# Whole tiles of adj by turns on two DMA queues, in place of half tiles on both

## The chip, the cores and the metric

The kernel runs on one core of one Trainium2 chip. The metric is the device time of one execution in microseconds (us), lower is better. The core has TensorE (PE in the profile, its weight loads PEld), VectorE (DVE), ScalarE (ACT), GpSimd (POOL) and SyncE (SP). Transfers are issued by SyncE, ScalarE and GpSimd, each into a queue of its own (q1 is SyncE's, q10 ScalarE's), and 16 DMA engines carry them out.

## What is computed

Two graph layers over N = 4096 nodes with 128 features, both with the same dense 4096 x 4096 float32 matrix adj (64 MB) and a layer norm ahead:

```python
h = jnp.maximum(_layernorm(x, axis=-1), 0.0)
x = x + _L0_gnn_ref(h, adj, L0_gnn_weight, L0_gnn_bias)
h = jnp.maximum(_layernorm(x, axis=-1), 0.0)
x = x + _L1_gnn_ref(h, L1_gnn_context, adj, ...)

# L0: a hyperbolic layer
h = proj(mobius_matvec(weight, x, C_IN), C_IN)
h = proj(mobius_add(h, hyp_bias, C_IN), C_IN)
support_t = adj @ logmap0(h, C_IN)
h = proj(expmap0(support_t, C_IN), C_IN)
return proj(expmap0(jax.nn.relu(logmap0(h, C_IN)), C_OUT), C_OUT)

# L1: attention over the edges of adj
left, right = in_fts @ w_left + b_left, in_fts @ w_right + b_right
logits = left[:, None] + right[None, :]
logits = jnp.where(logits >= 0, logits, 0.2 * logits)
logits = jnp.where(adj_tensor <= 0.0, -jnp.inf, logits)
return jax.nn.relu(jax.nn.softmax(logits, axis=-1) @ relation)
```

## The kernel before

It works in two parts. The first reads adj once, multiplies with it (layer 0) and keeps only the sign of each entry as an int8 mask in SBUF. The second computes layer 1 from that mask and doesn't touch adj.

The first part goes through NC = 8 chunks of 512 rows of adj (output nodes), and in a chunk through NC = 8 tiles (g = 0 to 7) of 512 columns. A tile is 512 x 512 float32, 1 MB. It is loaded into one of XSLOTS = 4 slots of `loaded` by four transfers of 256 KB, one for each quarter b of the partitions (quarter b is partitions 32 b to 32 b + 31, and takes columns 128 b to 128 b + 127 of the tile). Each transfer reads 512 runs of 512 bytes. `LOW` is quarters 0 and 1 (partitions 0 to 63), `HIGH` quarters 2 and 3 (64 to 127).

When all four have landed (semaphore `adj_in` of the slot), VectorE turns the tile in four blocks with 32 x 32 transposes (L975, `turn_block`, 0.69 us each) into four slots of `turned`. TensorE multiplies each block (L671), and ScalarE takes the signs of two blocks at a time (L829), which counts up `half_signed`. VectorE may overwrite a block's slot when it is multiplied and signed. The slot of `loaded` is free for tile g + 4 when tile g is turned.

Who asks for tile g + 4: SyncE's program `load` (L347) waits for `half_signed` to show tile g signed and then issues quarters 0 and 1 (L354). ScalarE issues quarters 2 and 3 (`load_high`, L719) in its own program, right behind its second sign of tile g, without a wait. The first four tiles of chunk 0 are loaded by SyncE alone, all four quarters in the order 0, 2, 1, 3, and the context (4 MB) after them, also by SyncE. An engine's program goes on when its issue has been taken; while an issue is held back, what stands behind it in that engine's program waits.

Between the tiles stand small transfers of 64 KB: at tile 4 the finished rows of two chunks earlier are stored (`store_x1`, L324), at tile 7 the rows of x for the chunk before are loaded into `xk` (`load_x`, L331), LOW by SyncE, HIGH by ScalarE. GpSimd (L553) waits for xk, and VectorE's statistics (L1093), among the last tile's blocks, wait for GpSimd.

Of the kernel before, what the change touches and what calls it, by code (L numbers as in the profile page):

```python
# [52 lines left out]
XT_AHEAD = 4  # L53
BESIDE = 8
STORE_AT, LOAD_AT = 4, 7
LOW, HIGH = range(NQ // 2), range(NQ // 2, NQ)

MIN_NORM2 = 1e-30
# [20 lines left out]
def bass_two_graph_layers(nc, x, adj, weight, bias, context, w_common, w_left, b_left, w_right, b_right, out):  # L79
# [3 lines left out]
    NC = N // CH  # L83
# [4 lines left out]
    with ExitStack() as ctx:  # L88
# [179 lines left out]
        adj_n = adj.rearrange("(s r p) (g b j) -> s g b p r j", r=CH // Q, p=Q, b=NQ, j=L * Q)  # L268

        def pick(view_, c):  # L270

            if isinstance(c, int):
                return view_[c]
            v = view_[bass.ds(c, 1)]
            names = "abdefg"[:len(v.shape) - 1]
            return v.rearrange(f"z {' '.join(names)} -> (z {names[0]}) {' '.join(names[1:])}")
# [28 lines left out]
        def by_l(t, l, j=None):  # L305

            v = t.rearrange("p (s l) d -> p l s d", l=L)[:, l]
            return v if j is None else v[:, j * L:(j + 1) * L]
# [12 lines left out]
        def store_x1(eng, p, blocks):  # L321
            eng.wait_ge(x1_ready, p + 1)
            for b in blocks:
                eng.dma_start(out_n[p, b], xk[b * Q:(b + 1) * Q]).then_inc(x1_stored, 16)  # L324

        def load_x(eng, p, blocks):
            if p:
                eng.wait_ge(x1_stored, p * (16 * NQ))
                eng.wait_ge(h2_ready, p)
            for b in blocks:  # L330
                eng.dma_start(xk[b * Q:(b + 1) * Q], x_n[p, b]).then_inc(xk_loaded, 16)  # L331
# [4 lines left out]
        @block.sync  # L336
        def _(sp):
            def load_nodes(t, src, into, blocks):
                for l in range(L):
                    for b in blocks:  # L340
                        sp.dma_start(by_l(t, l)[b * Q:(b + 1) * Q], src[l, b]).then_inc(into[l], 16)
            load_nodes(x_in, x_l, x_in_sem, LOW)

            for l in range(L):
                sp.wait_ge(x_in_sem[l], 16 * NQ)

            def load(c):  # L347

                for g in range(NC):
                    first_tiles = c == 0 and g < XSLOTS  # L350
                    if not first_tiles:
                        sp.wait_ge(half_signed, c * TH + HALVES * (g - XSLOTS + 1))
                    for b in (0, 2, 1, 3) if first_tiles else LOW:
                        sp.dma_start(loaded[b * Q:(b + 1) * Q, g % XSLOTS], adj_n[c, g, b]).then_inc(  # L354
                            adj_in[g % XSLOTS], 16)
                    if c == 0 and g == XSLOTS - 1:
                        load_nodes(cx, cx_l, cx_in, range(NQ))
                    if g == STORE_AT and c >= 2:
                        store_x1(sp, c - 2, LOW)
                    if g == LOAD_AT and c >= 1:  # L360
                        load_x(sp, c - 1, LOW)

            def neg_left_row(c, parity):
                sp.dma_start(nl[parity], (nl_dram[c * L:(c + 1) * L] if isinstance(c, int) else
                                          nl_dram[bass.ds(c * L, L)]).rearrange("(a l) p -> a (l p)", a=1)
                             .broadcast_to([P, CH])).then_inc(nl_loaded[parity], 16)

            for c in range(NC):
                load(c)
            sp.wait_ge(nl_stored, 16 * NQ)  # L370

            sp.wait_ge(block_turned, NC * NK - (XSLOTS - 1) * L)
            neg_left_row(0, 0)
            store_x1(sp, NC - 2, range(NQ))
            load_x(sp, NC - 1, range(NQ))

            def rows_out(p):

                os = pick(out_n, p)

                for b in range(NQ):
                    sp.dma_start(x1k[b * Q:(b + 1) * Q], os[b]).then_inc(x1_loaded, 16)
                sp.wait_ge(y_ready, p + 1)
                for b in range(NQ):
                    sp.dma_start(os[b], y[b * Q:(b + 1) * Q]).then_inc(out_stored, 16)

            def chunk_of_phase_2(c, parity):
                sp.wait_ge(parts_ready, c * NC - NC)
                neg_left_row(c, parity)
                rows_out(c - 2)  # L390

            store_x1(sp, NC - 1, range(NQ))
            neg_left_row(1, 1)
            sp.wait_ge(x1_stored, NC * 16 * NQ)
            sp.wait_ge(rest_ready, NK)
            sp.wait_ge(rest0_ready, NC)
            with sp.Fori(1, NC // 2) as pair:
                chunk_of_phase_2(pair * 2, 0)
                chunk_of_phase_2(pair * 2 + 1, 1)
            rows_out(NC - 2)  # L400
            for b in range(NQ):
                sp.dma_start(x1k[b * Q:(b + 1) * Q], out_n[NC - 1, b]).then_inc(x1_loaded, 16)
            for l in range(0, L, 2):
                sp.wait_ge(y_ready, NC + l // 2)
                for b in range(NQ):
                    sp.dma_start(out_n[NC - 1, b][:, l:l + 2], y[b * Q:(b + 1) * Q, l:l + 2]).then_inc(out_stored, 16)
            sp.wait_ge(out_stored, (NC + 1) * 16 * NQ)
# [299 lines left out]
        def _(act):  # L707
# [5 lines left out]
            act.dma_start(b_colv, bias.rearrange("(d a) -> d a", a=1)).then_inc(weights_in, 16)  # L713
            act.dma_start(bias_b, bias.rearrange("(a d) -> a d", a=1).broadcast_to([P, D])).then_inc(weights_in, 16)

            def load_high(rows, g):

                for b in HIGH:
                    act.dma_start(loaded[b * Q:(b + 1) * Q, g % XSLOTS], rows[g, b]).then_inc(adj_in[g % XSLOTS], 16)  # L719

            for l in range(1, L):
# [47 lines left out]
            def bias_part(k):  # L769

                if k >= XT_AHEAD:
                    act.wait_ge(xt_ready, k - XT_AHEAD + 1)
                nc.scalar.activation(fb[:, k % XT_AHEAD, :], hb, ACT.Copy, scale=sv[:, 14, k:k + 1]).then_inc(
                    fb_ready, 1)
# [39 lines left out]
            def signs(c, parity):  # L814
                number = isinstance(c, int)
                acc_of[0] = acc[1 - parity]
                steps = {}
                if c >= 1:
                    copy, squares, tanh, _ = post_steps(c - 1)
                    steps = {0: copy, 4: squares, 9: tanh}  # L820
                if c >= 2:
                    steps[2] = post_steps(c - 2)[3]
                if c == NC - 1:
                    steps[7] = exponentials
                mc = mask[:, c] if number else mask[:, bass.ds(c, 1)].rearrange("p o k i -> p (o k) i")
                for half in range(TH):
                    act.wait_ge(block_turned, c * NK + HB * (half + 1))
                    slots = half % HALVES * HB
                    nc.scalar.activation(mc[:, half * HB:(half + 1) * HB, :], turned[:, slots:slots + HB, :],  # L829
                                         ACT.Sign).then_inc(half_signed, 1)  # L830
                    if number and c == 0:
                        for k in range(XT_AHEAD + half * HB, min(NK, XT_AHEAD + (half + 1) * HB)):
                            bias_part(k)
                    if half in steps:
                        steps[half]()
                    if half % HALVES == HALVES - 1:
                        tile = half // HALVES + XSLOTS
                        if tile < NC:
                            load_high(adj_n[c], tile)
                        elif c < NC - 1:  # L840
                            load_high(adj_n[c + 1], tile - NC)
                        if tile == STORE_AT and c >= 2:
                            store_x1(act, c - 2, HIGH)
                        if tile == LOAD_AT and c >= 1:
                            load_x(act, c - 1, HIGH)
# [6 lines left out]
            for c in range(NC):  # L852
                signs(c, c % 2)
# [414 lines left out]
```

## Time and profile before

| | |
|---|---|
| three timed runs | 627.44, 631.89, 632.68 us; median 631.89 |
| the profiled execution | 626.75 us, its span 625.0 us |
| busy, share of the span | PE 503.0 us (80%), DVE 510.6 (82%), ACT 420.0 (67%), POOL 234.4 (38%) |
| adj loads issued | SyncE 136, ScalarE 120, 256.0 KB each, 9.8 and 9.0 us from issue to landing |
| packets of q1 and q10 | 49.69 MB and 34.35 MB |

Busy times are of the whole program and mix the two parts; a share of the DMA engines above 1 means that the recorded times of packets overlap on an engine. Durations all come from the one profiled execution.

### The profile page before, as it was taken

The numbers are of one execution on the slowest core, as the hardware profiler recorded it, in microseconds if no ns is written. First come the engines' busy times: TensorE is split into PE (matmuls) and PEld (weight loads), VectorE is DVE, ScalarE is ACT, GpSimd is POOL, SyncE is SP. The second block draws the span as 40 slices with busy tenths as digits, with TensorE's granted clock in tenths as the row PEclk, the third lists the DMA queues.
The fourth block names the chain that finished last, engine by engine and source line by source line (L and its number), as shares of the span: only waits on it lengthen the run. The fifth ranks groups of instructions, "written<-read, shape, count | busy, mean of one in ns | idle before, by whom it ended". The sixth has DMA issues, their size and how long they took to land.

```text
span 625.0 us, 8712 instructions
## 1 busy us (share of the span) xinstructions
PE 503.0 (80%) x2695; PEld 313.2 (50%) x2695; DVE 510.6 (82%) x980; ACT 420.0 (67%) x554; POOL 234.4 (38%) x259
## 2 busy tenths in 40 slices
PE   0823999898989878896886565699999999999995
PEld 0721443332423332342332444488787878787874
DVE  3896987766857676683676999999999999999994
ACT  1955876563746446463466958498989898989881
POOL 4820047757556684532333886201111111010100
PEclk9975999998999899899799879989999999999999
DMA  6997999999999999999992010101010101011010
GB/s 151 225 221 145 185 259 282 276 254 274 232 273 240 242 232 239 268 235 194 241 258 71 5 34 1 35 18 35 18 35 18 34 17 34 17 34 34 0 34 17
DMA packets 164349, 84.59 MB, mean 135 GB/s; under 512 B 7344, under 2 KB 163248, under 8 KB 164320
## 3 DMA queue, kind: packets, MB, share of 16 engines
q1 hardware_dynamic: 94240, 49.69, 38.0%
q10 hardware_dynamic: 69712, 34.35, 26.6%
q0 software_dynamic: 368, 0.22, 0.2%
q8 instruction: 11, 0.18, 0.1%
q14 instruction: 18, 0.15, 0.1%
HBM read 80.02 MB, written 4.21 MB: 135 GB/s over the span
## 4 chain that ended last, share of the span: by engine, by line
DVE 44%; DMA 22%; issue 11%; ACT 7%; PE 6%; SPq 5%; POOL 3%; ACTq 2%; DVEq 1%; POOLq 0%
DMA xk<-in_x_dram 11%; DMA room<-in_adj_dram 10%; DVE room L1139 6%; DVE room L975 5%; DVE room L1185 5%; DVE mask L1139 5%; DVE mask L1185 4%; DVE room L1195 4%; PE ps L671 4%; ACT mask L829 3%; DVE mask L1195 3%; PE ps L697 3%; SPq L354 2%; SPq L331 2%; DVE h_room L1209 2%
## 5 line engine op out<-in xcount | busy, mean ns | idle before, releaser
L671 PE MATMUL ps<-room 128*128 128x512 f32 x512 | 246.4, 627 | 52.9 <-DVE room L975 32.3
L975 DVE STREAM_TRANSPOSE room<-room 128x512 f32<-128x512 f32 x256 | 167.8, 690 | 71.4 <-DMA room<-in_adj_dram 34.0
L829 ACT ACTIVATE mask<-room 128x1024 int8<-128x1024 f32 x128 | 132.5, 1052 | 120.0 <-DVE room L975 92.4
L671 PEld LDWEIGHTS ps<-room 128*128 128x128 f32 x512 | 95.1, 196 | 198.8 <-DVE room L975 108.9
L697 PE MATMUL ps<-room 128*128 128x258 f16 x1152 | 136.4, 279 | 31.7 <-DVE room L1195 31.7
L697 PEld LDWEIGHTS ps<-room 128*128 128x128 bf16 x1152 | 112.5, 99 | 54.3 <-DVE room L1195 37.3
L697 PE MATMUL ps<-room,mask 128*128 128x258 f16 x896 | 102.8, 275 | 9.5 <-DVE h_room L1209 6.3
L697 PEld LDWEIGHTS ps<-room,mask 128*128 128x128 bf16 x896 | 87.1, 98 | 24.1 <-DVE h_room L1209 7.7
L886 ACT ACTIVATE room<-mask 128x2048 bf16 (+1 forms) x36 | 68.5, 1903 | 16.8 <-PE ps L697 16.8
L606 POOL TENSOR_TENSOR h_room<-h_room 128x512 f32<-128x512 f32 x7 | 9.8, 1405 | 145.4 <-DVE post L1220 145.4
L886 ACT ACTIVATE mask<-mask 128x2048 bf16 (+1 forms) x28 | 53.3, 1903 | 5.4 <-PE ps L697 5.4
L471 POOL TENSOR_TENSOR mask<-mask,h_room 128x2048 f32<-128x2048 f32 x8 | 36.2, 4526 | 50.4 <-DVE room L1064 50.1
L1185 DVE TENSOR_TENSOR room<-room 128x2048 bf16<-128x2048 bf16 x36 | 47.8, 1328 | 2.9 <-ACT room L886 1.9
L480 POOL TENSOR_TENSOR mask<-mask 128x1024 f32<-128x1024 f32 (+6 forms) x56 | 44.8, 801 | 4.0
L1185 DVE TENSOR_TENSOR mask<-mask 128x2048 bf16<-128x2048 bf16 x28 | 34.7, 1238 | 1.1
L918 ACT ACTIVATE h_room<-ps,factors 128x258 f32<-128x258 f32 x32 | 13.9, 471 | 30.8 <-PE ps L697 17.9
L539 POOL TENSOR_TENSOR post<-post,powers 128x8 f32<-128x8 f32 x8 | 13.3, 1668 | 46.9 <-DVE post L1087 46.9
L1139 DVE TENSOR_SCALAR room<-room,r_col 128x512 bf16<-128x512 f32 x42 | 28.6, 723 | 0.0
L553 POOL TENSOR_TENSOR xk<-relu_u,xk 128x512 f32<-128x512 f32 x8 | 10.2, 1270 | 40.6 <-DMA xk<-in_x_dram 40.6
L1195 DVE TENSOR_SCALAR room<-room 128x2048 bf16<-128x2048 bf16 x36 | 25.4, 705 | 0.0
L895 ACT ACTIVATE room<-room,r_col 128x512 bf16<-128x512 f32 x38 | 25.1, 708 | 0.0
L1194 DVE TENSOR_SCALAR room<-room 128x2048 bf16<-128x2048 bf16 x36 | 24.6, 683 | 0.2
(168 smaller groups left out, 526.8 us busy)
## 6 DMA issues: line engine op xcount, KB each, us to landing
room<-in_adj_dram SPq DMA_DIRECT2D x136, 256.0 KB, 9.8
room<-in_adj_dram ACTq DMA_DIRECT2D x120, 256.0 KB, 9.0
mask<-in_L_gnn_context_dram SPq DMA_DIRECT2D x16, 256.0 KB, 10.5
h_room<-out_dram SPq DMA_DIRECT2D x32, 64.0 KB, 2.6
out_dram<-h_room SPq DMA_DIRECT2D x28, 64.0 KB, 1.7
out_dram<-xk SPq DMA_DIRECT2D x20, 64.0 KB, 8.3
xk<-in_x_dram SPq DMA_DIRECT2D x18, 64.0 KB, 8.6
mask<-in_x_dram ACTq DMA_DIRECT2D x8, 128.0 KB, 6.5
```

What stands on the lines that cost most here:

```text
L471: side(tt(room_of, cx[:, ks, :], v_rows[:, w, :].unsqueeze(1).broadcast_to([P, BESIDE, C]), ALU.mult))
L480: side(tt(dst, room_of[:, :, 0:n], room_of[:, :, n:2 * n], ALU.add))
L671: pe.matmul(acc[parity], xt[:, k, :], turned[:, k % TSLOTS, :], start=(k == 0), stop=(k == NK - 1)).then_inc(block_multiplied, 1)
L697: mm = pe.matmul(ps[:, 2 * t + w, 0:GW], part[slot(c, g)][:, kk, t * P:(t + 1) * P], G[w][:, k, :], start=(k == 0), stop=(k == NK - 1))
L829: nc.scalar.activation(mc[:, half * HB:(half + 1) * HB, :], turned[:, slots:slots + HB, :], ACT.Sign).then_inc(half_signed, 1)
L886: nc.scalar.activation(neg[slot(c, g)], mc[:, g * L:(g + 1) * L, :], ACT.Relu, scale=4.0).then_inc(edges_ready, 1)
L895: ins = nc.scalar.activation(pos[slot(c, g)][:, kk, :], nl[parity], ACT.Sign, scale=-1.0, bias=r_col[:, k:k + 1])
L975: v.transpose(turned[:, k % TSLOTS, :].rearrange("p (l b i) -> p b l i", l=L, b=NQ), loaded[:, g % XSLOTS, :, l * Q:(l + 1) * Q].rearrange ...
L1139: ins = v.tensor_scalar(pos[slot(c, g)][:, kk, :], nl[parity], r_col[:, k:k + 1], -1.0, ALU.is_le, ALU.add)
L1185: v.tensor_tensor(pos_g, pos_g, neg_g, ALU.add).then_inc(coded, 1)
L1194: v.tensor_scalar(neg_g, pos_g, 3.0, None, ALU.is_equal)
L1195: v.tensor_scalar(pos_g, pos_g, 4.0, None, ALU.is_ge).then_inc(parts_ready, 1)
```

## The change

Each tile from the fifth on is loaded by one queue: SyncE issues all four quarters of the even tiles in the order 0, 2, 1, 3, ScalarE all four of the odd ones in the order 2, 0, 3, 1. Waits, slots, semaphores and the first four tiles are as before; SyncE still waits for `half_signed` at an odd tile, with nothing to issue behind it but the xk loads of tile 7.

```diff
@@ -53,6 +53,7 @@
 XT_AHEAD = 4
 BESIDE = 8
 STORE_AT, LOAD_AT = 4, 7
+BY_SYNC, BY_ACT = (0, 2, 1, 3), (2, 0, 3, 1)
 LOW, HIGH = range(NQ // 2), range(NQ // 2, NQ)
 
 MIN_NORM2 = 1e-30
@@ -350,7 +351,7 @@
                     first_tiles = c == 0 and g < XSLOTS
                     if not first_tiles:
                         sp.wait_ge(half_signed, c * TH + HALVES * (g - XSLOTS + 1))
-                    for b in (0, 2, 1, 3) if first_tiles else LOW:
+                    for b in BY_SYNC if first_tiles or g % 2 == 0 else ():
                         sp.dma_start(loaded[b * Q:(b + 1) * Q, g % XSLOTS], adj_n[c, g, b]).then_inc(
                             adj_in[g % XSLOTS], 16)
                     if c == 0 and g == XSLOTS - 1:
@@ -713,9 +714,9 @@
             act.dma_start(b_colv, bias.rearrange("(d a) -> d a", a=1)).then_inc(weights_in, 16)
             act.dma_start(bias_b, bias.rearrange("(a d) -> a d", a=1).broadcast_to([P, D])).then_inc(weights_in, 16)
 
-            def load_high(rows, g):
-
-                for b in HIGH:
+            def load_odd(rows, g):
+
+                for b in BY_ACT:
                     act.dma_start(loaded[b * Q:(b + 1) * Q, g % XSLOTS], rows[g, b]).then_inc(adj_in[g % XSLOTS], 16)
 
             for l in range(1, L):
@@ -835,10 +836,12 @@
                         steps[half]()
                     if half % HALVES == HALVES - 1:
                         tile = half // HALVES + XSLOTS
-                        if tile < NC:
-                            load_high(adj_n[c], tile)
+                        if tile % 2 == 0:
+                            pass
+                        elif tile < NC:
+                            load_odd(adj_n[c], tile)
                         elif c < NC - 1:
-                            load_high(adj_n[c + 1], tile - NC)
+                            load_odd(adj_n[c + 1], tile - NC)
                         if tile == STORE_AT and c >= 2:
                             store_x1(act, c - 2, HIGH)
                         if tile == LOAD_AT and c >= 1:
```

Of ScalarE's program, chunk 1 from tile 4's blocks on (L829 two signs, L719 an adj quarter, L331 xk, L793 and L794 squares of layer 0). Before:

```order
89 L719 DMA room<-in_adj_dram 32x16x128 x2
90 L829 ACTIVATE mask<-room 128x1024 x2
91 L719 DMA room<-in_adj_dram 32x16x128 x2
92 L829 ACTIVATE mask<-room 128x1024
93 L793 ACTIVATE ps<-ps 128x512
94 L794 ACTIVATE ps<-relu_u 128x512
95 L829 ACTIVATE mask<-room 128x1024
96 L719 DMA room<-in_adj_dram 32x16x128 x2
97 L829 ACTIVATE mask<-room 128x1024 x2
98 L719 DMA room<-in_adj_dram 32x16x128 x2
99 L331 DMA xk<-in_x_dram 32x4x128 x2
```

And now, where the same operations are one line further down (L830, L720, L332, L794, L795):

```order
84 L830 ACTIVATE mask<-room 128x1024 x3
85 L720 DMA room<-in_adj_dram 32x16x128 x4
86 L830 ACTIVATE mask<-room 128x1024
87 L794 ACTIVATE ps<-ps 128x512
88 L795 ACTIVATE ps<-relu_u 128x512
89 L830 ACTIVATE mask<-room 128x1024 x3
90 L720 DMA room<-in_adj_dram 32x16x128 x4
91 L332 DMA xk<-in_x_dram 32x4x128 x2
92 L830 ACTIVATE mask<-room 128x1024 x2
```

Two issues behind every two signs have become four behind every four, and the xk loads stand behind four of them.

Of SyncE's program, from chunk 0's fifth tile to the end of chunk 2 (L354 adj, L331 xk loads, L324 stores). Before:

```order
L354 DMA room<-in_adj_dram 32x16x128 x24
L331 DMA xk<-in_x_dram 32x4x128 x2
L354 DMA room<-in_adj_dram 32x16x128 x10
L324 DMA out_dram<-xk 32x4x128 x2
L354 DMA room<-in_adj_dram 32x16x128 x6
L331 DMA xk<-in_x_dram 32x4x128 x2
```

And now:

```order
L355 DMA room<-in_adj_dram 32x16x128 x24
L332 DMA xk<-in_x_dram 32x4x128 x2
L355 DMA room<-in_adj_dram 32x16x128 x12
L325 DMA out_dram<-xk 32x4x128 x2
L355 DMA room<-in_adj_dram 32x16x128 x4
L332 DMA xk<-in_x_dram 32x4x128 x2
```

The same number of adj loads lies between two xk loads, sixteen, but the store stands behind twelve of them (tiles 0, 2 and 4, all quarters) where it stood behind ten (tiles 0 to 4, two quarters each).

## Rows read from the trace of the kernel before

**Rows 1.** The page, part 2: DMA busy in tenths and GB/s, in 40 slices of 15.6 us.

```profile
DMA  6997999999999999999992010101010101011010
GB/s 151 225 221 145 185 259 282 276 254 274 232 273 240 242 232 239 268 235 194 241 258 71 5 34 1 35 18 35 18 35 18 34 17 34 17 34 34 0 34 17
```

**Rows 2.** Windows: busy us and instructions of each engine, clock, DMA share, GB/s.

```profile
core 0: us, PE busy (x) PEld busy (x) DVE busy (x) ACT busy (x) POOL busy (x), PEclk, DMA share, GB/s
22.00:32.00 10.00, 7.13 (x53) 5.96 (x51) 8.17 (x12) 10.00 (x25) 9.57 (x9) 1.00 1.22 224
85.00:95.00 10.00, 9.94 (x27) 4.29 (x25) 7.47 (x15) 6.08 (x7) 8.32 (x4) 1.00 1.20 288
157.00:165.00 8.00, 8.00 (x23) 3.81 (x22) 6.18 (x10) 6.53 (x10) 5.43 (x8) 1.00 1.20 207
82.50:332.50 250.00, 217.38 (x479) 85.63 (x478) 171.69 (x320) 136.34 (x169) 136.62 (x164) 0.97 1.20 249
338.00:625.00 287.00, 238.20 (x2054) 199.99 (x2052) 271.07 (x429) 227.47 (x274) 71.14 (x58) 0.97 0.09 23
```

**Rows 3.** Waits of DVE, 82.5 to 332.5 us: us in total, times, longest.

```profile
DVE room L975 <- DMA room<-in_adj_dram: 34.0, 25, 6.4
DVE room L975 <- ACT mask L829: 23.7, 14, 3.3
DVE stats L1093 <- POOL xk L553: 9.8, 6, 1.8
DVE room L975 <- PE ps L671: 9.6, 14, 2.4
```

**Rows 4.** The chain of waits, 150 to 205 us: start, us, what.

```profile
155.64 1.06 ACT mask L829
156.72 0.31 SPq L354
157.07 8.59 DMA room<-in_adj_dram
...
175.23 8.90 DMA xk<-in_x_dram
```

**Rows 5.** DMA queue, 22 to 32 us: packets, MB, share of 16 engines.

```profile
q1 hardware_dynamic: 4485, 2.23, 121.8%
```

**Rows 6.** DMA queues, 85 to 95 us (q1 is SyncE's, q10 ScalarE's).

```profile
q10 hardware_dynamic: 2917, 1.45, 60.7%
q1 hardware_dynamic: 2872, 1.42, 59.4%
```

**Rows 7.** DMA queues, 74 to 75 us.

```profile
DMA packets 431, 0.21 MB, mean 213 GB/s; under 512 B 15, under 2 KB 431, under 8 KB 431
...
q1 hardware_dynamic: 424, 0.21, 119.7%
q10 hardware_dynamic: 7, 0.00, 1.8%
```

**Rows 8.** DMA queues, 76.5 to 77.5 us.

```profile
DMA packets 429, 0.21 MB, mean 213 GB/s; under 512 B 14, under 2 KB 429, under 8 KB 429
...
q10 hardware_dynamic: 424, 0.21, 121.0%
q1 hardware_dynamic: 5, 0.00, 1.3%
```

**Rows 9.** Timeline, two slow and two fast issues: start, us, engine.

```profile
155.65 0.86 ACTq L719 DMA_DIRECT2D room<-in_adj_dram  x2
...
156.72 0.84 SPq L354 DMA_DIRECT2D room<-in_adj_dram  x2
...
86.08 2.17 ACTq L719 DMA_DIRECT2D room<-in_adj_dram  x2
87.16 1.74 SPq L354 DMA_DIRECT2D room<-in_adj_dram  x2
```

**Rows 10.** Waits of all engines: us in total, times, longest.

```profile
POOL xk L553 <- DMA xk<-in_x_dram: 40.6, 7, 11.3
```

## The prediction

> **What bounds the kernel now.** I read the page's forty slices first. The DMA line stands at 9 until slice 21 and falls to 0, 1 and 2 after it, and GB/s falls with it [rows 1]: the program has a first part that loads adj, and a second one that computes from what is on the chip. The change touches the first part alone. Its windows say more [rows 2]. From 82.5 to 332.5 us the DMA share is 1.20, the same as in the stretches in which the queues are visibly full, while PE, DVE and ACT are busy for 217, 172 and 136 of 250 us. The DMA engines never rest there, and the stretch lasts as long as its bytes at the rate they move: 250 us x 249 GB/s = 62.25 MB. From 338 to 625 us they have almost nothing to do, so those 287 us stay.
>
> The waits of VectorE, which turns the tiles, agree: in these 250 us it waits 34.0 us for adj to land, in 25 waits, 23.7 us for ScalarE's signs, 9.8 us for GpSimd and 9.6 us for TensorE [rows 3]. The chain of waits shows how they hang together: sign, SyncE's issue, 8.59 us of DMA until that tile has landed; 18 us on, an xk load of 8.90 us, then GpSimd and VectorE [rows 4]. Latency of 8 to 9 us for one 256 KB transfer is queueing: everything waits in line behind the same engines.
>
> The rate itself is not one number. With SyncE's queue alone (the first tiles, four quarters in the order 0, 2, 1, 3) it is 224 GB/s, with the share at 1.22, so full [rows 2, 5]. From 85 to 95 us both queues move equal amounts, 1.45 and 1.42 MB [rows 6], and the rate is 288. From 157 to 165 us it is 207 with a share of 1.20 [rows 2]. What differs is seen in single microseconds of a slow stretch: from 74 to 75 us 424 packets of SyncE's queue and 7 of ScalarE's, at 213 GB/s [rows 7]; from 76.5 to 77.5 us 5 and 424 [rows 8]. So the chip has two regimes in this kernel. In one, the two queues interleave, one writing partitions 0 to 63 and the other 64 to 127, at 288. In the other, one queue at a time is served, one half of the partitions at a time, at about 210. In the slow regime the issues go through at once (0.86 and 0.84 us for two), in the fast one they take 2.17 and 1.74 us, that is, they are held back by a full queue [rows 9]. Interleaving needs a deep backlog on both queues.
>
> How much of each? x at 288 and the rest at 210 (between 207 and 213) gives 249 for x = 0.50: 125 us that move 36.0 MB, and 125 us that move 26.25 MB.
>
> **The change, part by part.** Counts first: SyncE issues 136 adj loads and ScalarE 120, before and after, with the same bytes each, and the first four tiles are loaded as before. Nothing is removed. What moves is which half of the partitions a queue writes at a given moment, how many transfers come in a row (four per second tile in place of two per tile), and the depth that a tile finds.
>
> 1. Slow regime. One queue at a time is served, now with its quarters alternating between halves. That is the pattern of the first tiles on SyncE's queue: 224 GB/s [rows 2, 5] against 207 to 213. 26.25 MB / 224 = 117.2 us in place of 125: **-7.8 us**. Bounds: nothing (it stays at 210), and a gain that is larger if alternating halves from two queues pull these stretches into the fast regime.
>
> 2. Fast regime. Before, whatever the queues' positions, one writes low and the other high partitions. Now SyncE's tile goes low, high, low, high and ScalarE's high, low, high, low. They complement each other only if both are at the same quarter, or two apart; one quarter apart they write the same half together. Nothing in the code holds them in step: an odd tile is asked for when its slot is free, one tile later than the even one, and a queue that runs dry restarts at any offset; the xk loads and stores (64 KB) shift it by fractions. The trace of before has no stretch in which both queues write the same half. The nearest rows are one half at a time, 207 to 224; the other end is the 288 of complementary halves. I take 224 for the same half, since it is the value that alternating quarters reached, and equal bytes in either relation, since no offset is favoured: 18.0 MB / 288 + 18.0 MB / 224 = 62.5 + 80.4 = 142.9 us in place of 125: **+17.9 us**. Bounds: 0 (always complementary) and 36.0 / 224 = 160.7 us, +35.7 us (never).
>
> The Trainium skill's page SBUF — State Buffer, section "Door 1: The DMA port swizzle", says that partitions 0 to 63 sit on the eight even DMA ports and 64 to 127 on the eight odd ones, so that a transfer of 32 partitions reaches 8 of 16 ports, with an asymptote of 218 GB/s. The trace's 224 for one queue alone agrees nearly. By that figure the same-half stretches would take 18.0 / 218 = 82.6 us, an estimate 2.2 us above mine.
>
> 3. Bursts on ScalarE. Its sequencer now issues four in a row after every second tile, 27 times in the stretch. Held back, two take 2.17 us [rows 9], so four take about 4.3. Behind them stand the two signs of the next tile, behind these VectorE (four turned slots) and SyncE's next load. But the next tile lands no sooner than 1.05 MB / 288 = 3.6 us later, and four turns fit into the four slots without a new sign. So the burst ends before its signs are due, and I cost it at 0; the cover is the gap between landings. Upper bound 1 us a burst, 27 us, if a burst lasts over about 5 us. Per pair of tiles the sum of issue time is the same as before.
>
> 4. The xk loads. GpSimd waits 40.6 us for them in 7 chunks [rows 10], and VectorE's last tile of a chunk waits for GpSimd. Ahead of them stand four transfers on either queue now (tile 6 on SyncE's, tile 7 on ScalarE's) as before (two of each). 0, at most 1 us in each of 7 chunks on ScalarE's side.
>
> 5. Start and end. Tiles 4 to 6 of chunk 0 have landed long before VectorE gets there; 0. The second part: 0.
>
> **The sum** is -7.8 + 17.9 = +10.1 us on the profiled execution's 626.75 us (span 625.0), 636.9. That execution lies 5.1 us below the median of the three runs, 631.89 (627.44 to 632.68), so the forecast is **642.0 us**. About 1% (6 us) is also what a measurement of this kernel can tell from no change.
>
> **Rivals.**
> A, the halves meet well. An odd tile is asked for one tile's time after the even one, and while two queues share the engines each moves two quarters in that time, so ScalarE's tile would start when SyncE's is two quarters on, which is complementary. Then part 2 costs 0 and part 1 stays: -7.8, 624 us. If each queue's burst of four also keeps the backlog deep so that the fast regime holds three quarters of the time, the rate is 0.75 x 288 + 0.25 x 224 = 272, 62.25 / 272 = 228.9 us, -21, 611; it can't pass -34.0, the waits that there are [rows 3]. For it: the orders in the code are complementary in step. Against it: nothing holds the step, and the xk transfers shift it.
>
> B, no interleaving at all. Each queue holds one or two whole tiles, and whichever is in front is served alone. Everything at 224: 62.25 / 224 = 277.9 us, +27.9, 660 us. For it: in [rows 7, 8] the queues are already served one after the other while both have transfers issued. It decides where a queue's backlog runs out before its next even or odd tile is asked for; before, both queues held a share of every tile that was out. The bursts of part 3 would add to the same side.
>
> C, the rate doesn't depend on who writes where. Then all stays, 632 us. The Trainium skill's page DMA: Bandwidth & Descriptors, section "Rules for kernel authors", says that two transfers to disjoint halves of the partitions serialize and aren't worth doing, since both use the same 16 DMA engines. The trace speaks against it here: 288 with two halves together, 224 with one. What remains for no change is that gains and losses cancel: part 2 costs only 7.8 if complementary bytes are nearly 80% of the fast ones.
>
> **How the numbers follow.** Forecast, mixed offsets, +6 to +20: 0.38. B with its additions, above +20: 0.15. C, or cancelling: 0.20. A: 0.27. So faster 0.27, same 0.20, slower 0.53. The range leaves out the deeper end of A and what lies beyond B: 619 to 661. Because both signs hold much of the chance, the forecast's own range is 638 to 652.
>
> **What would show it.** In the windows between 82.5 us and the end of the loads the mean rate should be near 240 GB/s with the share still 1.2; stretches of both queues in equal amounts should show rates between 215 and 288 and not 288 alone; slow stretches should show 220 or more, not 207. VectorE's wait for adj should grow by about 10 us, and the part after the last turned tile should keep its 287 us. The prediction is wrong in its part 2 if the interleaved stretches keep 288; wrong in part 3 if VectorE's wait for ScalarE grows by more than 10 us; wrong in its frame if the DMA share falls below 1.1, because then the engines rest and bytes over rate no longer gives the time.

## The result: 659.0 us in place of 632.3, 4.65% slower

The changed kernel takes 659.0 us (median of 4 runs, 656.03 to 660.2), the kernel before 632.28 (median of 4, 627.44 to 636.43); the ratio is 1.0465, 95% interval 1.0415 to 1.0515. The forecast was slower, 642.0: the direction was right, and the step was 26.7 us where I had forecast 10. The time stands just inside the wide range (619 to 661), outside the narrower 638 to 652, and at the price of rival B.

The page of the changed kernel, part 2, DMA busy and GB/s in 40 slices (16.5 us each), answers to [rows 1]:

```profile
DMA  6995999999999999999999101010110101011010
GB/s 148 227 220 120 216 232 220 218 240 219 217 231 216 235 218 223 223 220 231 182 223 225 44 1 32 1 33 17 33 36 21 42 16 32 16 32 32 0 32 16
```

The share is as full as before while the loads last, and the rate, which swung between 185 and 282, is now flat at 216 to 240 but for one slice. Windows of the changed kernel (the columns of [rows 2]):

```profile
85.00:95.00 10.00, 7.66 (x18) 3.35 (x17) 5.56 (x11) 4.56 (x6) 8.06 (x3) 0.83 1.21 228
82.50:364.50 282.00, 222.40 (x476) 86.25 (x475) 170.48 (x319) 137.79 (x171) 136.56 (x164) 0.96 1.20 221
370.00:658.40 288.40, 242.05 (x2055) 201.91 (x2054) 271.60 (x430) 227.83 (x274) 71.54 (x58) 0.96 0.09 23
```

From 82.5 us to the end of the loads it is 282 us at 221 GB/s, with a share of 1.20: 62.3 MB, the same bytes as the 250 x 249 of before [rows 2]. A mean rate always gives its own time back, so that product proves nothing; what bears out the frame of the prediction is that the bytes and the share are those of before, and that the lost time lies here. The second part takes 288.4 us (287 before). Of the 33.4 us between the two spans (658.4 and 625.0), 32 lie in this stretch. Where [rows 2] had 288 from 85 to 95 us, there is 228 now.

What the queues do is seen in two pairs of microseconds. DMA queues of the changed kernel, 87 to 89 us (packets, MB, share):

```profile
DMA packets 903, 0.45 MB, mean 225 GB/s; under 512 B 24, under 2 KB 903, under 8 KB 903
...
q10 hardware_dynamic: 878, 0.44, 118.2%
q1 hardware_dynamic: 25, 0.01, 3.4%
```

And from 100 to 102 us:

```profile
DMA packets 895, 0.44 MB, mean 222 GB/s; under 512 B 28, under 2 KB 895, under 8 KB 895
...
q1 hardware_dynamic: 868, 0.43, 117.5%
q10 hardware_dynamic: 27, 0.01, 4.2%
```

In these windows one queue is served alone, then the other. To have one number for it I counted the packet records of the stretch in half microseconds:

| | before | after |
|---|---|---|
| the weaker queue moved 40% of the bytes or more | 45% of the time, 267 GB/s | 14%, 230 GB/s |
| it moved 10 to 40% | 51%, 236 GB/s | 40%, 219 GB/s |
| one queue nearly alone, over 90% | 4%, 188 GB/s | 46%, 218 GB/s |

So the pattern of [rows 7, 8], which were read at 74 to 77.5 us, ahead of the stretch, was rare in the stretch before, and it is nearly half of it now. The time in which both queues share evenly has shrunk to a third, and even then the rate is 230, not 288.

Waits of VectorE in the stretch, answering to [rows 3]:

```profile
DVE room L978 <- DMA room<-in_adj_dram: 60.2, 29, 6.4
DVE room L978 <- ACT mask L830: 43.7, 21, 4.9
DVE room L978 <- PE ps L672: 3.5, 9, 0.6
DVE stats L1096 <- POOL xk L554: 2.1, 4, 1.1
```

The wait for adj has grown by 26.2 us, and the wait for ScalarE by 20.0; the experiments must say which of the two carries the 32 us.

### The profile page after: what moved, and what is told of

The parts are those of the page before. It is cut to its first block, busy times and chain, and to the rows that moved or that the text cites. A ratio compares the mean times of both kernels' runs of the same rounds, so it can differ in the third digit from the quotient of the medians.

```text
span 658.4 us, 8735 instructions
## 1 busy us (share of the span) xinstructions
PE 511.6 (78%) x2695; PEld 315.3 (48%) x2695; DVE 510.1 (77%) x980; ACT 420.1 (64%) x554; POOL 234.4 (36%) x259
## 4 chain that ended last, share of the span: by engine, by line
DVE 38%; DMA 17%; issue 11%; ACTq 10%; ACT 9%; PE 9%; SPq 4%; POOL 2%; DVEq 1%; POOLq 0%
DMA room<-in_adj_dram 8%; DVE room L1142 5%; ACTq L720 5%; DVE room L1188 5%; DVE mask L1142 4%; ACT mask L830 4%; DMA out_dram<-xk 4%; PE ps L672 4%; PE ps L698 4%; DVE room L978 4%; DVE mask L1188 3%; DVE room L1198 3%; ACTq L332 3%; DMA xk<-in_x_dram 3%; DVE mask L1198 3%
## 5 line engine op out<-in xcount | busy, mean ns | idle before, releaser
L672 PE MATMUL ps<-room 128*128 128x512 f32 x512 | 251.2, 636 | 78.4 <-DVE room L978 58.0
L830 ACT ACTIVATE mask<-room 128x1024 int8<-128x1024 f32 x128 | 133.6, 1052 | 151.9 <-DVE room L978 99.5
L698 PE MATMUL ps<-room 128*128 128x258 f16 x1152 | 141.5, 285 | 29.3 <-DVE room L1198 29.3
L698 PEld LDWEIGHTS ps<-room 128*128 128x128 bf16 x1152 | 114.9, 101 | 54.8 <-DVE room L1198 35.3
L698 PE MATMUL ps<-room,mask 128*128 128x258 f16 x896 | 101.2, 273 | 9.5 <-DVE h_room L1212 6.4
L607 POOL TENSOR_TENSOR h_room<-h_room 128x512 f32<-128x512 f32 x7 | 9.8, 1406 | 146.4 <-DVE post L1223 146.4
L612 POOL TENSOR_TENSOR h_room<-h_room 128x512 f32<-128x512 f32 x7 | 10.2, 1462 | 32.3 <-ACT h_room L914 32.3
```

The lines of the kernel that those rows point to most:

```text
L672: pe.matmul(acc[parity], xt[:, k, :], turned[:, k % TSLOTS, :], start=(k == 0), stop=(k == NK - 1)).then_inc(block_multiplied, 1)
L698: mm = pe.matmul(ps[:, 2 * t + w, 0:GW], part[slot(c, g)][:, kk, t * P:(t + 1) * P], G[w][:, k, :], start=(k == 0), stop=(k == NK - 1))
```

## The experiments

Three theories stood after the result. **N**: the two queues no longer run together; each tile sits in one queue and is served alone. **H**: the queues do run together in part, but collide in the same half of the partitions. **S**: ScalarE's bursts of four issues hold back signs. In the expectations D stands beside them: the depth of both queues' backlogs decides, whatever the halves. Orders such as 0, 2 / 1, 3 are SyncE's quarters / ScalarE's. Medians of 4 runs each (e10: 10), against the kernel before on the same chip.

| | edit | us | before | ratio |
|---|---|---|---|---|
| e1 | before, 0, 2 / 1, 3 | 634.6 | 627.7 | none |
| e2 | before, 0, 3 / 2, 1 | 656.7 | 627.7 | 1.047 (1.042 to 1.052) |
| e3 | all on SyncE's queue | 660.4 | 627.7 | none |
| e4 | before, three tiles out | 663.5 | 627.7 | 1.059 (1.053 to 1.065) |
| e5 | e2, columns as before | 655.4 | 632.2 | 1.039 (1.028 to 1.050) |
| e6 | after, halves in blocks | 681.4 | 632.2 | 1.078 (1.067 to 1.090) |
| e7 | before, SyncE asks when turned | 615.3 | 632.2 | 0.976 (0.966 to 0.986) |
| e8 | after, SyncE asks when turned | 659.2 | 632.2 | 1.043 (1.033 to 1.053) |
| e9 | e7, 0, 2 / 1, 3 | 660.2 | 629.4 | 1.051 (1.045 to 1.057) |
| e10 | e7, 0, 2 / 3, 1 | 630.6 | 629.4 | 1.000 (0.996 to 1.005) |
| e11 | after, pairs asked together | 670.6 | 629.4 | 1.065 (1.059 to 1.072) |

Of e1 and e3 one run of four lay 1.5% or more below the other three (622.5 beside 633.4 to 636.6, 647.4 beside 660.4 to 661.2), so no interval is given for them; their windows and waits are of one of the three. For e7 the interval is a gain of 1.4 to 3.4%.

### e3: one queue

```diff
-                    for b in BY_SYNC if first_tiles or g % 2 == 0 else ():
+                    for b in BY_SYNC:
...
-                for b in BY_ACT:
+                for b in ():
```

> The changed kernel, but SyncE issues the odd tiles as well (order 0, 2, 1, 3), ScalarE none: one queue carries adj, and ScalarE's bursts are gone. Theory N (the changed kernel lost because its two queues are served one after the other nearly all the time): one queue at 224 GB/s is about what it already had, 62.25 / 224 = 278 us, 655 to 662, the same as the changed kernel's 659. Rival S (the loss is ScalarE's bursts of four issues, which hold back signs): VectorE's wait for ScalarE falls from 43.7 us to under 20 and the time falls by 10 us or more below the changed kernel, to 635 to 648.

Windows of e3, with the first tiles for comparison, and then its waits of VectorE over the whole program:

```profile
82.50:364.00 281.50, 224.68 (x484) 86.39 (x482) 171.25 (x322) 140.43 (x172) 136.62 (x164) 0.96 1.20 222
22.00:32.00 10.00, 6.56 (x48) 5.55 (x48) 8.08 (x14) 10.00 (x25) 9.50 (x9) 1.00 1.22 223
```

```profile
DVE room L978 <- DMA room<-in_adj_dram: 96.1, 46, 7.5
...
DVE room L978 <- ACT mask L830: 3.0, 2, 1.8
```

222 GB/s in the stretch, 223 in the first tiles, and in this execution (661.2 us) the time of the changed kernel (660.2). VectorE's wait for ScalarE has gone down to 3.0 us, and here nothing is won by it: the wait moved to the transfers, 96.1 us. That speaks for N and against S. It doesn't settle it alone: the fourth run, at 647.4, is 11.6 us below the changed kernel's median, about what S had asked for, and no trace of it shows why. e4 and e9 below speak against S without that doubt.

### e4: three tiles out

```diff
-                        sp.wait_ge(half_signed, c * TH + HALVES * (g - XSLOTS + 1))
+                        sp.wait_ge(half_signed, c * TH + HALVES * (g - XSLOTS + 2))
...
-                        if tile < NC:
-                            load_high(adj_n[c], tile)
+                        if c == 0 and tile == XSLOTS:
+                            pass
+                        elif tile - 1 < NC:
+                            load_high(adj_n[c], tile - 1)
...
-                            load_high(adj_n[c + 1], tile - NC)
+                            load_high(adj_n[c + 1], tile - 1 - NC)
```

> The kernel before, but each tile is asked for one tile later by both queues (three tiles out at most in place of four). Theory D (interleaving needs a deep backlog on both queues): the stretches at 288 shrink, mean rate from 249 towards 225, 645 to 665, and issues are no longer held back. Rival: the DMA engines are never idle anyway and the rate depends on the halves alone, so three tiles out give the same, 632 within 5.

The window of e4's stretch, and its wait for adj:

```profile
82.50:364.00 281.50, 220.76 (x476) 84.38 (x476) 172.15 (x324) 138.99 (x170) 136.87 (x164) 0.96 1.18 222
```

```profile
DVE room L977 <- DMA room<-in_adj_dram: 96.4, 48, 5.8
```

Half tiles on both queues, the halves as before, and yet 222 GB/s and 663.5 us. The DMA share is still 1.18, so the engines are busy nearly all the time; they are busy at the slower rate. The time with both queues at 40% or more fell to 16%, and one queue is nearly alone for 47%, at 211 GB/s. So in this kernel running together needs the fourth tile in the queues. S has nothing to explain here: there are no bursts of four, and e4's list of VectorE's waits has no wait for signs of the first part at all, yet it is as slow as the changed kernel.

### e2 and e5: crossed orders, and which side of a transfer matters

```diff
-                    for b in (0, 2, 1, 3) if first_tiles else LOW:
+                    for b in (0, 2, 1, 3) if first_tiles else (0, 3):
...
-                for b in HIGH:
+                for b in (2, 1):
```

> The kernel before, but SyncE's queue takes quarters 0 then 3 and ScalarE's 2 then 1: in step the halves differ, and each queue alternates between the halves as in the changed kernel. Theory H: where both are in step it stays at 288, where one queue is served alone it rises from about 210 to the 224 of alternating quarters; if they stay in step 625, if offsets drift 635 to 645. Theory D: 632 within 5. If the changed kernel lost because its queues alternate halves at drifting offsets, this one loses too.

The window of e2's stretch:

```profile
82.50:358.00 275.50, 221.07 (x472) 83.71 (x470) 168.48 (x316) 134.61 (x166) 136.75 (x164) 0.96 1.22 224
```

29 us are lost with half tiles on both queues, outside everything that I had expected of e2. Here both queues do run together (about 64% of the time), and the rate while they do is only 227 GB/s. That is theory H in a kernel of its own. It also means that running together isn't enough: the halves that meet must differ. e5 adds an exchange of columns to e2, `(0, 3, 2, 1)[b]` in place of `b` on the side of adj:

> The crossed order of e2 on the side of the partitions (SyncE's queue writes quarters 0 then 3, ScalarE's 2 then 1), but each queue reads the columns of adj that it read before (128 columns number 0 and 1 of a tile by SyncE, 2 and 3 by ScalarE): quarters 1 and 3 of the partitions hold each other's columns, so adj is computed with its columns permuted and the output isn't the reference's. It tells the two things apart that a quarter means, where it is written and where it is read. Theory P (the partitions written decide): as e2, 652 to 661. Theory M (the addresses read in HBM decide): as the kernel before, 625 to 634.

```profile
82.50:358.00 275.50, 222.87 (x480) 85.34 (x479) 171.30 (x319) 137.28 (x169) 136.59 (x164) 0.96 1.21 225
```

The row is e5's window; 655.4 us, the same loss. Between the partitions that are written and the columns that are read, it is the partitions that decide. The Trainium skill's page SBUF — State Buffer, section "Door 1: The DMA port swizzle", has the rule for this: each half of the partitions sits on its own eight of 16 ports, with about 218 GB/s for eight. The 221 to 227 GB/s of the colliding kernels lie 1 to 4% above that figure.

### e1: the same half in step

```diff
-                    for b in (0, 2, 1, 3) if first_tiles else LOW:
+                    for b in (0, 2, 1, 3) if first_tiles else (0, 2):
...
-                for b in HIGH:
+                for b in (1, 3):
```

> The kernel before, each tile still shared by both queues and issued at the same moments, but SyncE's queue takes quarters 0 and 2 and ScalarE's 1 and 3, so that in step both write the same half of the partitions (0 with 1, then 2 with 3). Theory H (two queues run faster than one only while they write different halves): no stretch at 288 is left where they are in step, both regimes near 222, 62.25 MB / 222 = 280 us in place of 250, about 655 to 662. Theory D (only the depth of both queues' backlogs decides, whatever the halves): the backlogs are those of before, so 632 within 5. Mixed offsets would give 640 to 650.

```profile
82.50:338.00 255.50, 217.08 (x479) 85.23 (x478) 171.65 (x320) 136.93 (x169) 136.64 (x164) 0.97 1.20 243
```

The row is e1's window: 243 GB/s, hardly less than 249, and 634.6 us, which is no clear difference. By H as I had put it this kernel had to lose most, and e2 nothing. I had the step wrong. From the packet records, SyncE's n-th quarter of a tile lands 1.7 us after ScalarE's n-th in the kernel before (median, within about 0.1; 1.9 in e1, 1.8 in e2), and a quarter takes 1.8 us when two queues share the engines. So the queues run one transfer apart: in e1 SyncE's 0 runs beside ScalarE's 3 (different halves), in e2 SyncE's 0 beside ScalarE's 1 (the same). The next three kernels test this.

### e7, e9, e10: both queues in step

e7 changes one wait, so that both queues ask at the same moment:

```diff
-                        sp.wait_ge(half_signed, c * TH + HALVES * (g - XSLOTS + 1))
+                        sp.wait_ge(block_turned, c * NK + L * (g - XSLOTS + 1))
```

> The kernel before, but SyncE asks for tile g + 4 when tile g is turned (the slot is free then), no longer when its signs are taken as well, about 1.1 us earlier and at the moment when ScalarE asks for its half. Theory D (a deeper backlog on both queues at the same time keeps them interleaving): more time at 288, mean rate from 249 to 255 or more, 5 to 12 us faster, 616 to 624. If the backlog of the later half doesn't matter: 628 within 4.

The window of e7's stretch, its waits of VectorE, and its queues from 100 to 110 us:

```profile
82.50:316.00 233.50, 206.96 (x474) 84.03 (x473) 170.41 (x319) 135.45 (x168) 136.68 (x164) 0.99 1.21 265
```

```profile
DVE room L975 <- ACT mask L829: 41.9, 25, 5.8
DVE room L975 <- PE ps L671: 12.0, 16, 1.6
DVE room L975 <- DMA room<-in_adj_dram: 2.6, 5, 0.9
```

```profile
DMA packets 5847, 2.92 MB, mean 292 GB/s; under 512 B 185, under 2 KB 5846, under 8 KB 5846
...
q10 hardware_dynamic: 2932, 1.46, 59.8%
q1 hardware_dynamic: 2914, 1.44, 59.5%
```

615.3 us, 2.4% below the kernel before (1.4 to 3.4%), just below what I had expected, and the best of all. Rate 265; VectorE waits only 2.6 us for adj in the whole program, and what it waits for now is ScalarE (41.9 us). That is nearly the 43.7 us of the changed kernel, in the fastest of all kernels. The queues share evenly about 65% of the time (45 before), and SyncE's quarters land 0.4 us before ScalarE's: in step. The edit makes SyncE's backlog deeper and puts the queues in step at once; which of the two gives the gain isn't separated. With that known, e9 and e10 put the same and different halves beside each other.

```diff
-                    for b in (0, 2, 1, 3) if first_tiles else LOW:
+                    for b in (0, 2, 1, 3) if first_tiles else (0, 2):
...
-                for b in HIGH:
+                for b in (1, 3):      # e9
+                for b in (3, 1):      # e10
```

> e7 (both queues ask for their halves of a tile at the same moment, and run in step) with SyncE's queue taking quarters 0 then 2 and ScalarE's 1 then 3: in step both write the low half, then both the high one. Theory H: the stretches of both queues fall to about 222, mean under 225, 650 to 662 in place of e7's 615. If only changing halves costs and not the collision: the same as e10. If halves don't matter in step: 615.

> e7 with SyncE's queue taking quarters 0 then 2 and ScalarE's 3 then 1: in step they write different halves at all times, and each changes halves with every transfer. Theory H in its simple form (in step is enough): 612 to 620 as e7. If the 16 engines are spread over a transfer's length, so that some of them have changed halves while others haven't, it loses part: 630 to 645, but less than e9.

The window of e9's stretch, its queues from 100 to 110 us, and its waits of VectorE over the whole program:

```profile
82.50:362.00 279.50, 221.79 (x474) 86.88 (x473) 170.75 (x318) 135.62 (x169) 136.51 (x164) 0.95 1.21 221
```

```profile
DMA packets 4664, 2.33 MB, mean 233 GB/s; under 512 B 141, under 2 KB 4663, under 8 KB 4663
...
q1 hardware_dynamic: 2331, 1.16, 60.1%
q10 hardware_dynamic: 2332, 1.15, 60.0%
```

```profile
DVE room L975 <- ACT mask L829: 71.8, 30, 5.6
DVE room L975 <- DMA room<-in_adj_dram: 22.8, 19, 2.2
```

The window and the queues of e10:

```profile
82.50:328.00 245.50, 207.82 (x464) 82.41 (x462) 166.98 (x312) 132.44 (x164) 135.31 (x161) 0.98 1.22 247
```

```profile
DMA packets 4758, 2.38 MB, mean 238 GB/s; under 512 B 140, under 2 KB 4757, under 8 KB 4757
...
q1 hardware_dynamic: 2380, 1.19, 60.6%
q10 hardware_dynamic: 2377, 1.18, 59.7%
```

Three kernels that differ in the halves alone, each against the kernel before on its chip: 0.976 (615.3, a queue keeps its half), 1.000 (630.6, different halves in step, changing with every transfer), 1.051 (660.2, the same half in step). e9 has both queues active in equal amounts and gains nothing from it: 221 GB/s is the rate of one queue alone. Its waits also show what a wait for signs can mean: VectorE waits 71.8 us for ScalarE and 22.8 for adj, e4 not at all for the signs and 96.4 for adj, and both take 660 to 664 us. ScalarE's issues stand between its signs, and in e9 one adj issue takes 1.91 us in the median where it takes 0.44 in e4. So where issues are held back, the wait for the transfers shows up as a wait for ScalarE. e10 lies between. Its likeliest reason is that the 16 engines aren't at the same transfer at the same time (by the packet records, the first engine's end and the last one's of one transfer lie some 1.1 us apart from 85 to 95 us of before, where a quarter lands every 1.8 us, and some 1.8 us apart in e10, where one lands every 2.2), so some have changed halves while others haven't; that is argued, not shown.

### e6, e8, e11: variants of the changed kernel

```diff
-BY_SYNC, BY_ACT = (0, 2, 1, 3), (2, 0, 3, 1)
+BY_SYNC, BY_ACT = (0, 1, 2, 3), (2, 3, 0, 1)
```

> The changed kernel with other orders: 0, 1, 2, 3 on SyncE's queue and 2, 3, 0, 1 on ScalarE's, so that a queue stays in one half for two quarters. Theory N (what the change lost is that the queues are served together at all; both kinds of quarters are then one queue at a time): 659 again, 654 to 663. Theory H (the loss is quarters that collide in the same half because the queue changes halves with every transfer): half as many changes of half, 5 to 15 us faster, 644 to 654.

```profile
22.00:32.00 10.00, 7.42 (x53) 6.57 (x53) 8.07 (x21) 10.00 (x25) 8.70 (x9) 1.00 1.22 213
82.50:385.00 302.50, 231.97 (x475) 90.06 (x474) 171.51 (x322) 138.95 (x171) 136.56 (x164) 0.92 1.20 207
```

The rows are e6's first tiles and its stretch: 207 GB/s, and 681.4 us. Neither theory gave this. The first tiles are the cleanest comparison, since SyncE's queue loads them alone: with two quarters of one half in a row it has 213 GB/s, with alternating quarters 224 [rows 2]. In the stretch it is 207 against 221. So e6 isolates the gain that part 1 of the prediction had: 62.25 MB at 207 are 301 us, at 222 280 us, and the two kernels lie 22 us apart.

e8 gives the changed kernel e7's wait:

> The changed kernel with the same earlier wait on SyncE for the even tiles. Theory N: the tiles still enter the queues one after the other, so a microsecond of depth gives back little, 650 to 659. If the changed kernel only lacked depth, most of its 27 us come back: 632 to 645.

```profile
82.50:362.00 279.50, 224.35 (x471) 88.81 (x471) 171.91 (x320) 137.10 (x170) 136.56 (x164) 0.92 1.22 223
```

The row is e8's window. 223 GB/s and 659.2 us, at the upper edge of what N allowed: the wait that is worth 17 us with half tiles on both queues is worth nothing with whole tiles by turns.

e11 holds SyncE's even tile back until the odd tile's slot is free:

```diff
-                        sp.wait_ge(half_signed, c * TH + HALVES * (g - XSLOTS + 1))
+                        sp.wait_ge(half_signed, c * TH + HALVES * (g - XSLOTS + (1 if g % 2 else 2)))
```

> The changed kernel, but SyncE asks for an even tile one tile later, when the slot of the following odd tile is free too, so that both queues ask for a tile each at the same moment, with their orders complementary in step; the even tile's backlog is one tile shallower. Theory N with phase (asking together is what makes the queues interleave): time in which both move about equal amounts rises from 14% to over 40% and the rate above 235, 640 to 652. Rival (depth counts more than the moment): 660 to 675.

```profile
82.50:375.00 292.50, 234.04 (x491) 98.20 (x491) 175.79 (x334) 144.51 (x179) 137.89 (x165) 0.89 1.11 216
```

The row is e11's window. 670.6 us, 216 GB/s with a share of 1.11: the engines begin to run dry, and the time of equal sharing rose only to 20%. The moment of asking doesn't help where it costs depth. The rival was right.

## Why the prediction came out as it did

**The frame** was right: the same bytes move in the stretch, the share stays at 1.20, so that the rate gives the time, and the second part stays (288.4 us).

**Part 1** (one queue at a time with alternating quarters runs at 224 in place of about 210) was right in mechanism and nearly in size: 221 to 223 in e3 and in the changed kernel, 207 in e6. But the picture of the kernel before on which it was weighed, half of the time at 288 and half with one queue alone at 210, was too sharp: by the count, one queue was nearly alone for 4% of the stretch, and for 51% the queues shared unevenly, at 236 GB/s.

**Part 2 failed**, in its premise. It was right that quarters in the same half collide at the rate of one queue (e9: 221, I had taken 224), and that this comes from the partitions (e5). But I kept the fast regime's 36.0 MB as bytes that still move on both queues together and priced only the collision of half of them, +17.9 us. In fact the queues mostly stopped running together: 45% of the time before, 14% after, and the changed kernel's 221 GB/s is what e3 has with one queue (222). My own sentence "Interleaving needs a deep backlog on both queues" [rows 9] should have made me price this. Before, each tile that is out puts two transfers into either queue; now it puts four into one and none into the other. That this is why they stopped is argued, not shown; e4 shows how little margin there was: with three tiles out in place of four the kernel before falls to 222 GB/s as well. And running together would not have been enough: in the changed kernel both queues also change halves, and where the same halves meet that alone costs as much (e2, 656.7 us while running together). At 221 the 36.0 MB take 163 us and not 142.9, and 26.25 MB take 118.8 and not 117.2: +37.9 - 6.2 = +31.7, against 32 measured in the stretch. So the failed term is the +17.9 us of part 2; it came to about +38.

**Part 3** (bursts at 0) was wrong in its cover, by its own sign of being wrong, while no run shows that its price was. Timeline of ScalarE's burst for tile 5 of chunk 2 in the changed kernel, start and duration:

```profile
135.77 2.17 ACTq L720 DMA_DIRECT2D room<-in_adj_dram  x2
...
137.98 2.58 ACTq L720 DMA_DIRECT2D room<-in_adj_dram  x1
...
140.58 2.02 ACTq L720 DMA_DIRECT2D room<-in_adj_dram  x1
142.65 1.06 ACT L830 ACTIVATE mask<-room 128x1024 int8<-128x1024 f32 x1 [3.50 <-issue]
143.84 0.71 DVE L978 STREAM_TRANSPOSE room<-room 128x512 f32<-128x512 f32 x1 [3.14 <-ACT mask L830]
```

The burst runs from 135.77 to 142.60, 6.8 us and not 4.3; the next signs wait 3.50 us for it and VectorE 3.14 us for them. Over the stretch VectorE's wait for ScalarE rose by 20.0 us, past the 10 that I had named as what would refute this part. Yet three of e3's four runs, without a single burst, take as long, and e4 and e9 take the same 660 to 664 us with none and with 71.8 us of such waits. While the transfers set the pace, a wait for signs stands in place of a wait for adj. The one run of e3 at 647.4 leaves open whether the bursts cost something beyond that. **Part 4** (xk) cost nothing, as forecast: VectorE's wait for GpSimd is 2.1 us in the stretch, against 9.8 before.

**The rivals.** B, no interleaving at all, is near to what happened, and its sum, +27.9 us, is within 5 us of the stretch and 1.2 of the medians. I gave it 0.15. A's picture of complementary halves had little time to matter, and e10 shows that it would have gained nothing: with both queues in step, complementary and changing halves with every transfer, the time is that of the kernel before. C was refuted by e9 and e10: who writes where changes the time by 30 us.

## What to carry to other kernels

When two queues feed the same engines, look at which of them moves packets in single microseconds, not at the DMA share: here it read 1.2 at 207 and at 288 GB/s alike. Then count over the whole stretch: two chosen microseconds had shown me a pattern that held for 4% of it. Where transfers write 32 partitions each, as here, split each tile between the queues by fixed halves of the partitions, 0 to 63 on one and 64 to 127 on the other, and keep both backlogs deep; a deep backlog with the wrong halves (e2) and the right halves with a shallower one (e4) were 29 and 36 us slower. Let a queue ask at the earliest event that frees its slot: one wait on the turn in place of the signs gave 2.4%.

## What the runs showed of the hardware beyond that

- Two queues that each keep their half move 288 to 292 GB/s over 10 us (before and e7) and 265 over e7's whole stretch; two queues in step on the same half 221 over e9's; one queue alone 222 to 224 with alternating quarters (e3 and the first tiles) and 213 with two of one half in a row (e6's first tiles).
- With whole tiles by turns, or with three tiles out, the queues are served one after the other for nearly half of the time (878 packets of one beside 25 of the other in 2 us). With four tiles out and half of each on either queue, they share evenly for 45% of the time and more (about 80% in e10). The Trainium skill's page DMA: Bandwidth & Descriptors, section "Queues, rings and completion order", has each engine take turns between its queues packet by packet; the evenly shared stretches agree, while the 2 us with 878 packets beside 25 don't look like it, although both queues had transfers issued that hadn't landed.
- How deep the backlog must be, and what in the chip holds the order of arrival, stays open: the runs show only that four tiles out are enough with half tiles on both queues, three are not, and four whole tiles by turns are not.
